# Three weight transfers of an attention and mixture-of-experts kernel issued after the tokens' gather, and two small gathers after the output rows

## The reference

```python
x = x + xattn(layernorm(x), ctx, Wq, bq, Wk, bk)      # x: (4, 256, 256)
...
logits = tokens @ gate_weight.T;  top1 = argmax(logits)          # 1024 tokens, 8 experts
ranks  = cumsum(onehot(top1)) - 1;  keep those with rank < 160
hmid = gelu(einsum('ech,ehi->eci', dispatch, wi))     # wi: (8, 256, 1024)
eout = einsum('eci,eih->ech', hmid, wo)               # wo: (8, 1024, 256)
out  = x + combine(eout, softmax weight of the chosen expert)
```

## Time and profile before

| | us |
|---|---|
| median of 3 runs (lowest, highest) | 112.29 (111.95, 114.25) |
| the profiled execution's own time | 111.59 |
| its span, first to last instruction | 109.9 |

### The profile page before, as it was taken

The page is one execution under the profiler, slowest core; times in us unless marked ns, Lnnn a source line. Parts: engine busy times, 40 slices in busy tenths (PEclk is TensorE's granted clock), DMA queues, the critical chain, the costliest instruction groups (busy, mean ns, idle before and its releaser), DMA issues.

```text
span 109.9 us, 2011 instructions
## 1 busy us (share of the span) xinstructions
PE 102.0 (93%) x744; PEld 89.8 (82%) x744; DVE 34.6 (31%) x149; ACT 32.9 (30%) x95; POOL 33.3 (30%) x69
## 2 busy tenths in 40 slices
PE   5999999998899999999999999999999999999900
PEld 5885887877699789998998998579999899888700
DVE  0037987995810146400600400230030020023110
ACT  4138777977252303241041041003204104100000
POOL 5704675274770930000520300312011021031530
PEclk9999999999999999999999999999999999999999
DMA  2899999999991799999999999520001001001100
GB/s 78 268 301 364 336 299 424 430 418 405 415 375 73 198 359 400 333 389 422 427 418 422 431 427 429 251 85 5 0 0 41 0 6 48 0 0 46 57 3 3
DMA packets 7714, 25.77 MB, mean 235 GB/s; under 512 B 912, under 2 KB 4245, under 8 KB 5656
## 3 DMA queue, kind: packets, MB, share of 16 engines
q1 hardware_dynamic: 6680, 23.39, 56.1%
q0 software_dynamic: 880, 2.12, 5.0%
q10 hardware_dynamic: 144, 0.13, 0.6%
HBM read 21.14 MB, written 4.76 MB: 236 GB/s over the span
## 4 chain that ended last, share of the span: by engine, by line
PE 88%; DVE 5%; issue 1%; another core or an unknown queue 1%; POOL 1%
PE ps L884 75%; PE ps L925 4%; PE ps L979 3%; PE ps L888 2%; PE ps L881 2%; PE ps L1050 2%; DVE shared L644 2%; DVE rows L591 1%; POOL out L397 1%; DVE y_end L852 0%; DVE logits L602 0%; DVE slot L633 0%; DVE rows L668 0%; DVE val L618 0%
## 5 line engine op out<-in xcount | busy, mean ns | idle before, releaser
L884 PE MATMUL ps<-wo_sb,shared 128*32 128x128 f32 (+2 forms) x320 | 36.6, 337 | 0.2 <-issue 0.2
L884 PE MATMUL ps<-shared,wi_sb 128*128 128x160 f32 x244 | 34.6, 299 | 0.0
L884 PEld LDWEIGHTS ps<-wo_sb,shared 128*32 128x32 f32 (+1 forms) x320 | 29.4, 142 | 5.2 <-issue 1.1
L884 PEld LDWEIGHTS ps<-shared,wi_sb 128*128 128x128 f32 x244 | 33.6, 190 | 0.1
L509 ACT ACTIVATE shared<-ps 128x480 f32<-128x480 f32 (+1 forms) x24 | 12.5, 526 | 48.7 <-PE ps L884 43.1
L390 POOL DMA_INDIRECT out<-y,got x9 | 8.9, 993 | 53.9 <-DVE y L833 39.8
L833 DVE SCALAR_TENSOR_TENSOR y<-ps,share,got 128x256 f32<-128x256 f32 x9 | 4.4, 484 | 46.7 <-PE ps L884 46.7
L354 POOL DMA_INDIRECT slots_dram<-rows,slot x8 | 8.0, 1002 | 6.1 <-DVE slot L633 3.8
L884 PE MATMUL ps<-shared 128*128 128x256 f32 (+1 forms) x28 | 9.2, 482 | 0.0
L884 PE MATMUL ps<-attended,shared 128*128 128x274 f32 x32 | 8.5, 402 | 0.0
L884 PEld LDWEIGHTS ps<-shared 128*128 128x128 f32 x28 | 6.1, 230 | 1.9 <-issue 1.1
(11 more groups left out here) (94 smaller groups left out, 79.0 us busy)
## 6 DMA issues: line engine op xcount, KB each, us to landing
wi_sb<-in_wi SPq DMA_DIRECT2D x8, 1024.0 KB, 13.1
wo_sb<-in_wo SPq DMA_DIRECT2D x8, 1024.0 KB, 12.1
slots_dram<-fill SPq DMA_DIRECT2D x1, 1300.0 KB, 12.7
shared<-in_xT SPq DMA_DIRECT2D x2, 512.0 KB, 6.9
out<-rows SPq DMA_DIRECT2D x4, 256.0 KB, 7.5
got<-slots_dram SPq DMA_DIRECT2D x1, 780.0 KB, 5.3
got<-slots_dram SPq DMA_DIRECT2D x4, 130.0 KB, 2.7
shared<-in_x SPq DMA_DIRECT2D x2, 256.0 KB, 4.1
```

The costliest lines, as they stand in the source:

```text
L884: return nc.tensor.matmul(dst, lhsT, rhs, start=(k == 0), stop=last)
```

## The change

SyncE's program alone changes, and no instruction is added or removed. Three of the six weight transfers issued ahead of the wait for the scatters are issued after it: `wo` of expert 1 right behind the gather of expert 1's tile, and `wi` and `wo` of expert 2 behind all the gathers. The two `last_slots` go behind the four output transfers.

```diff
             weights(0)
-            weights(1)
-            weights(2)
+            first_weights(1)

             sp.wait_ge(scattered, 16 * NT)
             sp.dma_start(got[:, 1, :], by_rank[0:P, 1, :]).then_inc(got_one, 16)
+            second_weights(1)
             sp.dma_start(got[:, 0, :], by_rank[0:P, 0, :]).then_inc(got_zero, 16)
             sp.dma_start(got[:, 2:E, :], by_rank[0:P, 2:E, :]).then_inc(got_main, 16)
             sp.dma_start(rest[:, 1, :], by_rank[P:CAP, PER_STACK:E, :]).then_inc(rest_here[1], 16)
+            weights(2)
             weights(3)
-            last_slots(0)
-            last_slots(1)
             for b in range(B):
                 sp.wait_ge(full_rows, 2 * b + 2)
                 sp.dma_start(out_v[b], rows[:, 2 * b:2 * b + 2, 0:H]).then_inc(x1_out, 16)
+            last_slots(0)
+            last_slots(1)
```

More of the change, by code:

```diff
@@ L226, in turned_inputs, with first_weights, second_weights @@
                 sp.dma_start(xT[:, 2 * i:2 * i + 2, :, :], xT_v[i]).then_inc(xT_here[i], 16)
+            def first_weights(e):
+                sp.dma_start(wi_sb[:, e, :, :], wi_v[e]).then_inc(wi_here[e], 16)
+            def second_weights(e):
+                sp.dma_start(wo_sb[:, e, :, :], wo_v[e]).then_inc(wo_here[e], 16)
             def weights(e):
-                sp.dma_start(wi_sb[:, e, :, :], wi_v[e]).then_inc(wi_here[e], 16)
-                sp.dma_start(wo_sb[:, e, :, :], wo_v[e]).then_inc(wo_here[e], 16)
+                first_weights(e)
+                second_weights(e)
             def last_slots(r):
```

## The result

| | before | changed kernel |
|---|---|---|
| median of 4 runs each (lowest, highest), us | 112.16 (111.95, 114.25) | 114.62 (113.37, 115.11) |
| ratio, 95% interval | | 1.020 (1.011 to 1.029) |
| profiled execution's own time, us | 111.59 | 113.37 |
| its span, us | 109.9 | 111.6 |

Ratios compare the fast executions of both kernels, medians take all. The forecast was 111.8 us with a range to 113.7. The change costs 1.78 us in the profiled executions. The same kernel was run again later beside the kernel before (last experiments but one): 1.011 (1.005 to 1.017), so its lasting cost is 1 to 2%. The profiled run is the lowest of the four; the median lies 1.25 us above it, and the other three showed a mean granted clock of 0.972 to 0.982 where the profiled one has 0.999.

What follows compares the result with a forecast made beforehand. TensorE bounds the kernel, busy 93% of the span. From 111.59 us: -0.25 (idle before transposes), -0.9 (hole), +0.7 (expert 2's `wi`) gives 111.1; plus 0.70 for the median, 111.8 us, own range 110.9 to 112.7, wider range 110.8 to 113.7.

Steps and rivals of the forecast that it cites:

- Step 1: Scatters before the gather: without weights in front the last lands in 2.5 us instead of 3.66, 1.1 us earlier, at 34.4.
- hole of VectorE: VectorE idle 1.27 us from 25.83 without known releaser, read as an instruction fetch behind weights; TensorE idles 0.9 us before 28.01.
- Step 2: VectorE's early hole mostly goes: 1.0 of 1.27 us on VectorE and GpSimd, 0.9 on TensorE; scatters landed at 33.4.
- Step 3: Expert 2's `wi`, behind expert 1's `wo`, lands 11.1 us after the scatters, at 44.5; TensorE waits 0.7 us before mm1(2).
- filled hole: DMA engines only 75% busy from 36 to 38 us: a 0.5 us hole that the deferred transfer fills.
- Step 4: `rest` tile for dT(1) lands in 4.2 us beside expert 1's `wo`, at 37.6; TensorE's 0.4 us wait is not added.
- The large gather: Behind the same megabyte it frees VectorE 8.2 us after the scatters, at 41.6 as before; costs nothing.
- the idle 0.25 us before the transposes: TensorE's idle pieces at 38.40 and 39.02, before transposes of gathered tiles, vanish with earlier scatters: 0.25 us gained.
- The cover of expert 4's `wi`: It lands 24.7 us after the scatters, at 58.1 or 59.1, before mm1(4) at 61.24: cover 2 us, no cost.
- The output rows, the buffers `y` and the third tile: First output scatter moves to about 59, first `y` is free at 66, VectorE's third tile waits; TensorE has 3 us cover.
- B: Rival, 7%: at mm1(2) expert 2's `wi` lands at 47.35, scatters held by each other, nothing filled: +2.4, median 114.7 us.
- A: Rival, 35%: VectorE's hole stays, scatters land at 34.4, expert 2's `wi` at 45.5: +0.55, median 112.8 us.

Runs made afterwards that it cites:

- the early instruction transfer: Changed kernel plus 256 already-met waits in TensorE's program up to mm1(0), so its instruction transfer passes earlier: 111.03 against 109.95 us, ratio 1.011.
- the version above: Changed kernel with expert 1's `wo` issued behind expert 2's `wi`, small gathers still behind the output rows: 113.74 against 111.19 us, ratio 1.018.
- the small gathers alone: Kernel before with only the two small gathers (`last_slots`) moved behind the output rows: 111.1 against 111.19 us, ratio 0.9993.
- expert 1's weights both ahead: Changed kernel with expert 1's `wo` again issued ahead of the wait for the scatters: 110.94 against 111.19 us, ratio 0.9998.

## Why the prediction was wrong, step by step

The forecast put expert 2's `wi` at 44.5; it came at 46.68. That is 2.2 us, and it has two halves: the scatters landed 1.1 us later than forecast (34.49, not 33.4), and the transfer took 1.1 us more behind them (12.2, not 11.1).

Step 1 held. The last scatter took 2.46 us from its issue to SyncE's release (32.03 to 34.49), forecast 2.5, against 3.66 before; over all profiles with an emptied queue it was 2.45 to 2.71. But 3.66 was no price of a scatter. With all six weights in the queue SyncE was released at 35.51, 34.95 and 35.14 for last scatters issued at 31.85, 32.28 and 30.19: whatever the issue, 1.3 to 1.5 us after the weights' last packet (34.2, 33.5 and 33.9). With the queue emptied the release follows the issue, and so a hole of VectorE, which hardly moved the release before, now moves the scatters and every weight behind them.

Step 2 failed, the first half. "The hole should mostly go" rested on the hole lying under a full load, and on the price of a transfer beside weights, which belongs to another kind of transfer. The runs show the hole with the queue full and with it empty, and its absence with the queue full and with it empty. It is there in the profiles of before and after and in all four of the next chip, in its short form in two of the six and in its long form in four, and in none of the eight of the other two chips, whatever the order of the queue. That it is a fetch behind weights, as I read it, the record speaks against: in the changed kernel no instruction transfer passes from 24.4 to 30.5 us, gaps included, and in the repetition of the kernel before one passes at 25.5 us without a hole. What it is, and what picks the form, stays open: the trace names no engine of this core as the releaser. In its long form it took TensorE 1.8 us and not 0.9. That delay of TensorE was covered by the wait for `wi`; the delay of the scatters was not, since `wi` counts from them. So the long form probably has a share in the 1.75 us of the first pair: where neither kernel had the hole, mm1(2) started 0.59 us later than before and the profiled execution took 0.7 us more (110.8 against 110.1), with a wait of 2.2 us instead of 1.36, since TensorE comes earlier still. No run separates the two. By the Trainium skill's rule (Runtime: NRT & Kernel Launch, section Instruction fetch mechanics), which hides the fetches behind execution, the hole would not be a fetch and would stay; the trace agrees that it stays, and in the changed kernel that no fetch passes in it, and doesn't show why it is there.

Step 3 failed, the second half, by the size of one term. A mm1 weight with no megabyte ahead landed 9.0 us behind the scatters in the kernel before, and expert 2's own `wi` did so at 8.7, 9.0 and 9.9 us in the three versions with `wo` behind it, and at 9.7 with `wo` ahead of the wait: the base was right. With the megabyte ahead it was 12.1 to 12.4 in five of six profiles, and 11.7 in that with the early instruction transfer. Against the base on the same chip these five cost 3.2 to 3.7 us; I had put 2.1. Read at the median of the 16 DMA engines' ends, 7.8 us became 10.0 to 10.2: 2.2 to 2.3, near the forecast, filled hole included. But a transfer has landed when its slowest engine has ended, and that one came 1.1 to 1.6 us behind the fifteenth, where it was 0.5 us before. My ends of 10.7 and 11.85 had no room for it, since both took the load as even over the engines.

Step 4: the `rest` tile landed 3.3 us from its issue, forecast 4.2 (ends 3.0 and 5.5), and dT(1) didn't wait. Here the Trainium skill's rule that an engine takes packets from its queues in turn (DMA: Bandwidth & Descriptors, section Queues, rings and completion order) would have given 5.5 if each row had waited for one of the weight's. This trace doesn't show that. The large gather freed VectorE 8.1 us behind the scatters, forecast 8.2; the idle 0.25 us before the transposes went, as forecast.

The cover of expert 4's `wi` was wrong, and didn't count only because mm1(2) was late already. I gave it 24.7 us behind the scatters; it took 28.2, against mm1(4) at 61.24 or earlier. I had summed bytes, and the two small gathers passed for 0.27 MB. With them behind the rows and in front of that `wi` it took 28.0 to 28.5 us in the changed order and 29.7 in the version above, with them in front of the rows 27.0 and 26.5, with them behind it 25.1, close to my 24.7. The landings engine by engine tell why they weigh so much. A weight has 16 of them, a small gather five (in 26 of 28 cases, four in two): one when SyncE has issued it and the others at its end; so four engines seem to carry it. In the changed kernel expert 4's `wi` lands on twelve engines at 59.4 to 61.4 us and on four at 62.5 to 62.7. With that `wi` ahead of the small gathers the four latecomers are gone from it (all engines within 55.9 to 57.7) and stand at expert 5's `wi` instead (twelve at 62.6 to 64.2, four at 65.9 to 66.4). An estimate from these numbers: for its four engines the 0.27 MB weigh like a megabyte over 16, 2.5 us at 420 GB/s instead of the 0.6 that I had counted, which makes 24.7 into 26.6. The further 1.5 us where they stand behind the rows isn't explained by it. The output rows, the buffers `y` and the third tile came as forecast: 58.97 for 59, and 65.81 for 66.

Of the rivals it was B's mechanism at B's place, though not by B's way: its scatters "held by each other" did not occur, the landing of 46.7 fell short of its 47.2, and A's late scatters with a dearer `wi` made up the sum. A and B stood side by side, each worked out with the other term at its best; their union, the hole stays and `wi` is dear, had no chance of its own. The median was then 1.25 us above the profiled run, with lower clocks, and not 0.70.

## What to carry to other kernels

When loads are pushed behind an event, list every consumer's deadline in order and give each load its place by its own: here the same three megabytes cost 1 to 2% in the written order, and save 0.7 to 0.8% with `wo` behind the `wi` that is needed first and expert 4's `wi` no longer behind the small gathers that stand behind the rows. A wait that disappears uncovers the next deadline, so check the second one as if the first had been met. Price a deferred load by its slowest DMA engine, not by bytes over bandwidth, look how many engines carry a small one, and don't count a hole without a known releaser as a gain.

## What the runs showed of the hardware

**One engine carries a lag through the queue.** In the changed kernel the slowest of the 16 DMA engines ended 1.2 us behind the fifteenth at expert 2's `wi`, and again 1.2 us behind it at each of the next two transfers; in its repetition 1.6 us, three times. Fifteen engines are then done and the transfer has not landed.

**Small gathers in a full queue.** Two transfers of 130 KB held SyncE for 9.03 us in the changed kernel. In front of the rows they held it 1.2 us, but then the rows behind them did, 11.1 us: the place where SyncE stands moves with the order, and the DMA engines are full either way. What changes is when the next weight lands (25.1 to 29.7 us, above), because four engines have the small gathers to do as well. With nothing deferred (the small gathers alone) the same two held SyncE 3.9 us.

**The granted clock after an idle piece.** In one profile (expert 1's weights both ahead) TensorE idled 1.83 us from 28.92, and then ran at a lower granted clock over two stretches of 2 us (length, busy us (x count) by engine, PEclk, DMA share, GB/s):

```profile
29.00:31.00 2.00, 0.25 (x2) 0.28 (x3) 0.73 (x3) 0.07 (x1) 0.12 (x2) 1.00 0.20 71
31.00:33.00 2.00, 2.00 (x11) 2.00 (x11) 0.32 (x1) 0.43 (x2) 1.70 (x2) 0.62 0.18 67
33.00:35.00 2.00, 2.00 (x9) 2.00 (x9) 0.00 (x0) 1.16 (x1) 0.41 (x2) 0.53 0.18 67
35.00:37.00 2.00, 2.00 (x17) 2.00 (x16) 0.22 (x1) 0.57 (x1) 2.00 (x5) 1.00 0.73 177
```

That is the level of 1.2 GHz instead of 2.4 for most of that time; the 12 matmuls of mm1(0) took 2.86 us instead of 1.87. The changed kernel had an idle piece of 1.78 us at the same place in its profile and kept its clock.

The wait for `wi` can do the same. With the small gathers back in front of the rows TensorE idled 2.15 us until 46.07 and was busy from there:

```profile
45.00:47.00 2.00, 0.93 (x7) 0.93 (x8) 0.00 (x0) 0.00 (x0) 0.00 (x0) 1.00 1.02 430
47.00:49.00 2.00, 2.00 (x11) 2.00 (x10) 0.00 (x0) 0.48 (x1) 0.00 (x0) 0.58 1.02 430
49.00:51.00 2.00, 2.00 (x11) 2.00 (x10) 0.00 (x0) 0.09 (x1) 0.00 (x0) 0.57 1.04 369
```

mm1(2) took 6.29 us there, and 4.61 in the changed kernel. Without warm-up matmuls and in the repetition of the changed kernel the same wait (2.15 and 2.2 us) left the clock at 1.0 in the profile. So such an idle piece can cost another 1.7 us in some executions and nothing in others. That the executions of 114.2 to 115.1 us had such a stretch fits their mean clocks; none of them was profiled, so it isn't shown.
